# Two attention stages of a hybrid block, run one after the other or interleaved in one pipeline of 20 steps

## What is computed

```python
x = L0_attn_a_x                                    # (16, 512, 128)
x = x + attn_a(layernorm(x), w_qkv, w_out, b_out)  # 16 heads of 64
x = x + ffn(layernorm(x), W_r, W_k, W_v, mu_r, mu_k)
x = x + attn_b(layernorm(x), W_Q, W_K, W_V, W_O)   # 16 heads of 8, rotary
x = x + ffn(layernorm(x), W_r, W_k, W_v, mu_r, mu_k)

# attn_a, linear: q = softmax(q * 64**-0.5, over d), k = softmax(k, over tokens)
context = einsum('bnd,bne->bde', q, k); out = einsum('bde,bnd->bne', context, v)
return out @ w_out + b_out
# attn_b, full: q, k rotated
attn = softmax(einsum('bhqd,bhkd->bhqk', q, k) / sqrt(8)); ctx = einsum('bhqk,bhkd->bhqd', attn, v)
# ffn: x_prev is x shifted by one token
xr = mu_r * x + (1 - mu_r) * x_prev; xk = mu_k * x + (1 - mu_k) * x_prev
r = sigmoid(xr @ W_r); out = r * (square(relu(xk @ W_k)) @ W_v)
```

## Time and profile before

| | us |
|---|---|
| median of 3 runs (1165.8 to 1167.78) | 1166.34 |
| the profiled execution, its own time | 1165.81 |
| its span in the trace, first to last instruction | 1164.0 |
| busy: PE, ACT, DVE, POOL | 1019.4, 740.4, 676.2, 427.1 |

### The profile page before, as it was taken

The page is one execution under the profiler, slowest core; times in us unless marked ns, Lnnn a source line. Parts: engine busy times, 40 slices in busy tenths (PEclk is TensorE's granted clock), DMA queues, the critical chain, the costliest instruction groups (busy, mean ns, idle before and its releaser), DMA issues.

```text
span 1164.0 us, 23222 instructions
## 1 busy us (share of the span) xinstructions
PE 1019.4 (88%) x8311; PEld 582.1 (50%) x8311; DVE 676.2 (58%) x1620; ACT 740.4 (64%) x857; POOL 427.1 (37%) x338
## 2 busy tenths in 40 slices
PE   4999999999999999649998989998989999999993
PEld 3777777777777777532333333333333333333332
DVE  5788888888888888651334443444344434443334
ACT  3454444444444445318888888887888788878881
POOL 4555555555555555552302231223112311230000
PEclk9999999999999999969999999999999999999997
DMA  5011111111111111222332333233323332232211
GB/s 151 11 56 48 52 42 51 54 54 54 54 54 54 54 54 46 100 93 83 99 101 63 93 100 100 65 88 99 99 65 88 99 99 69 85 101 73 73 37 29
DMA packets 64184, 84.04 MB, mean 72 GB/s; under 512 B 12545, under 2 KB 39042, under 8 KB 64130
## 3 DMA queue, kind: packets, MB, share of 16 engines
q1 hardware_dynamic: 64130, 83.34, 23.8%
HBM read 28.77 MB, written 20.97 MB: 43 GB/s over the span
## 4 chain that ended last, share of the span: by engine, by line
PE 44%; DVE 20%; issue 17%; ACT 11%; POOL 3%; SPq 2%; DMA 2%; DVEq 0%; ACTq 0%; POOLq 0%
PE PS L1227 11%; ACT work L576 9%; PE PS L1208 9%; PE PS L945 5%; DVE work L609 4%; PE PS L950 3%; DVE q_sum L648 3%; PE PS L1056 3%; PE PS L952 3%; PE PS L951 3%; DVE st L591 2%; PE PS L1017 2%; DVE qk_norm L722 2%; PE PS L1065 1%; DMA qkv_back<-qkv_scratch 1%
## 5 line engine op out<-in xcount | busy, mean ns | idle before, releaser
L576 ACT ACTIVATE work<-PS 128x1024 f32<-128x1024 f32 x512 | 489.2, 1026 | 103.7 <-PE PS L1208 102.2
L1227 PE MATMUL PS<-work,v 128*32 128x512 f32 x2048 | 273.6, 606 | 1.1 <-ACT work L576 1.1
L1208 PE MATMUL PS<-q_st,k_st 32*128 32x512 f32 x1024 | 203.3, 498 | 40.6 <-ACT work L576 32.8
L1208 PEld LDWEIGHTS PS<-q_st,k_st 32*128 32x128 f32 x1024 | 80.1, 182 | 207.7 <-ACT work L576 167.9
L342 POOL TENSOR_TENSOR work<-work,q_rcp 128x1024 f32<-128x1024 f32 x64 | 122.3, 1912 | 89.8 <-DVE q_rcp L652 89.8
L331 POOL TENSOR_TENSOR rs<-ve,half_neg 128x4 f32<-128x4 f32 x64 | 66.1, 1033 | 240.2 <-DVE ve L602 240.2
L466 ACT ACTIVATE work<-PS 128x1024 f32<-128x1024 f32 x64 | 65.6, 1026 | 137.5 <-PE PS L952 137.5
L404 POOL TENSOR_TENSOR v<-qkv_back,one 128x512 f32<-128x512 f32 x16 | 16.6, 1040 | 265.7 <-PE PS L1227 265.7
L950 PE MATMUL PS<-work_r,h1h 128*128 128x512 f32 x256 | 109.1, 426 | 5.2 <-POOL h1l L337 3.4
L952 PE MATMUL PS<-work_r,h1l 128*128 128x512 f32 x256 | 102.0, 399 | 0.0
L951 PE MATMUL PS<-work_r,h1h 128*128 128x512 f32 x256 | 101.7, 397 | 0.0
(11 more groups left out here) (145 smaller groups left out, 1557.8 us busy)
## 6 DMA issues: line engine op xcount, KB each, us to landing
qkv_scratch<-qkv_sb SPq DMA_DIRECT2D x16, 768.0 KB, 3.2
qkv_back<-qkv_scratch SPq DMA_DIRECT2D x16, 768.0 KB, 4.6
work<-in_attn_a_x SPq DMA_DIRECT2D x32, 256.0 KB, 3.1
x_scratch<-x SPq DMA_DIRECT2D x16, 256.0 KB, 2.1
k_st<-k_hi SPq DMA_DIRECT2D x64, 64.0 KB, 2.1
k_st<-k_lo SPq DMA_DIRECT2D x64, 64.0 KB, 2.1
q_st<-q_hi SPq DMA_DIRECT2D x64, 64.0 KB, 2.1
q_st<-q_lo SPq DMA_DIRECT2D x64, 64.0 KB, 2.1
```

The costliest lines, as they stand in the source:

```text
L576: act.activation(probs[s % NC][:, 2 * t:2 * t + 2, :], PS[:, 2 * t:2 * t + 2, :], ACT.Exp).then_inc(s_exp.sem, 1)
L1208: mm = pe.matmul(PS[:, h, :], k_st[g % 2][rows, kc * P:(kc + 1) * P], q_st[g % 2][rows, :], start=True, stop=not guarded, tile_position=(3 ...
L1227: mm = pe.matmul(PS[32 * h:32 * h + 32, 4 + u, :], v_flat[p][:, kc, at:at + 32], probs[kc][:, h, :], start=(n % 8 == 0), stop=(n % 8 == 7) ...
```

## The change

Both halves become one loop (`fused`, 20 steps). Step i works on batch a = i (projections of attention A), s = i-1 (end of attention A, first feed-forward layer), l = i-2 (q, k, v of attention B, rotation, split), b = i-3 (scores and weighted values of attention B) and e = i-4 (its output, second feed-forward layer). Steps 3 to 15 have both a and b. Every step has 16 units. Unit n on PE is: one half of a projection (three products into the one bank 4), all four score tiles (banks 0 to 3) behind one wait, the weighing of the values of unit n-1 (bank 6), and then "the other product" of that unit, from a list written out by hand, in banks 4, 5 or 7. ACT does one exp of 128x512 and one of 128x2048 in a unit. Steps without b use four banks for the projections in turn; steps without a (16 to 18) make the scores in pairs, as before.

Because only eight banks exist, bank 4 serves the projections and six other products in a step; each is followed by a wait, ahead of the next projection, for the DVE instruction that empties it. q, k, v of attention B stay in SBUF (the copy back from DRAM goes; the store stays, for the branch of large norms). The mixtures of the feed-forward layers are now made from SBUF: ACT copies (`h_copy`), POOL subtracts (`difference`), DVE combines (`mix`). POOL squares k (was DVE), DVE takes relu (was ACT), DVE copies h1 and adds the rotation's parts (were ACT and POOL). The norms of q and k are judged in step 18; their branch now repeats attention B after the loop in the case of large norms only. E tiles of attention A have two buffers instead of four, and the exp results of attention B two instead of four.

```diff
-def over_batches(eng, step, n, tail, last=1):
...
+        def iterations(eng, step):
+            for i in range(5):
+                step(i, i % 2)
+            with eng.Fori(5, 13, 2) as i:
+                step(i, 1)
+                step(i + 1, 0)
+            for i in range(13, FUSED):
+                step(i, i % 2)
...
+            def exp_half(a, n, alone):
+                c, r = n // 4, n % 4
+                if r == 0:
...
+                    hold(act, c_mm, a, c - 1)
+                hold(act, ph_mm, a, n + 1)
+                bank = n % 4 if alone else 4
+                act.activation((EQ, EK)[r // 2][c % 2][:, (r % 2) * 512:(r % 2) * 512 + 512], PS[:, bank, :], ACT.Exp)\
+                   .then_inc(ph_exp.sem, 1)
+
+            def exp_scores(z, b, n):
+                hold(act, z["pv"], b, n - 1)
+                hold(act, z["s_mm"], b, n + 1)
+                act.activation(probs[n % 2], PS[:, 0:4, :], ACT.Exp).then_inc(z["s_exp"].sem, 1)
...
+            def proj_half(a, p, n, alone):
...
+                hold(pe, ph_exp, a, n - 3 if alone else n)
+                bank = n % 4 if alone else 4
...
+                halves(PS[:, bank, :], (h1h[p][:, tok], h1l[p][:, tok]), (wqk_hi[:, cols], wqk_lo[:, cols]))\
+                    .then_inc(ph_mm.sem, 1)
...
+            def scores(z, b, n):
+                g, kc = n // NC, n % NC
+                if kc == 0:
+                    stacks_there(z, b, g)
+                hold(pe, z["s_exp"], b, n)
+                for h in range(4):
+                    rows = slice(32 * h, 32 * h + 32)
+                    mm = pe.matmul(PS[:, h, :], k_st[g % 2][rows, kc * P:(kc + 1) * P], q_st[g % 2][rows, :],
+                                   start=True, stop=True, tile_position=(32 * h, 0))
+                mm.then_inc(z["s_mm"].sem, 1)
...
+                for n in range(16):
+                    if A:
+
+                        if B and n == 0:
+                            hold(pe, f1["relu"], l)
+                        if E and n == 3:
+                            hold(pe, z["ct_sb"], e)
+                        if B and n == 9 and there(a + 1):
+                            hold(pe, h1_sb, a + 1)
+                        if E and n == 11:
+                            hold(pe, f2["relu"], e)
+                        if B and n == 12:
+                            hold(pe, z["u_norm"], b, 2)
+                        if E and n == 13:
+                            hold(pe, f2["x"], e, 1)
+                        if B and n == 14:
+                            hold(pe, f1["relu"], s)
+                        proj_half(a, p, n, not B)
+                    if B and A:
+                        scores(z, b, n)
+                    if B and not A:
+                        scores_split(z, b, n)
+
+                    if B and n >= 1:
+                        weigh_values(z, b, n - 1, 1 - p)
+                    if E and n == 0:
+                        weigh_values(z, e, 15, p)
...
```

More of the change, by code:

```diff
@@ L78, in sig @@
             return Signal(ctx, nc, name, per)
[L82 to L96, removed]
@@ L230, in hybrid_block, with batches @@
+        def batches(eng, step):
+            step(0)
+            with eng.Fori(1, NB, 1) as j:
+                step(j)
         block = ctx.enter_context(nc.Block())
@@ new lines, in _ @@
+            pool.wait_ge(a_known.sem, a_known.at(0))
+            with pool.If(pool.value_load(bounded_a[0:1, 0:1], min_val=0, max_val=1) == 1):
+                iterations(pool, fused)
+            with pool.Else():
+                for j in range(NB):
+                    guarded_a(j)
+                    if there(j + 1):
+                        guarded_head(j + 1, (j + 1) % 2)
+            pool.wait_ge(b_known.sem, b_known.at(0))
+            with pool.If(pool.value_load(bounded_b[0:1, 0:1], min_val=0, max_val=1) == 0):
+                batches(pool, guarded_b)
@@ new lines, in guarded_a, with guarded_b @@
+            def guarded_a(j):
+                for c in range(NC):
+                    exp_q(j, c)
+                    exp_k(j, c)
+                t_copy(j)
+                m_copy(j)
+                h_copy(ffn[0], j)
+                gates(ffn[0], j)
+                hold(act, qkv_st, j - 1)
+                for c in range(NC):
+                    p_copy(j, c)
+            def guarded_b(i):
+                for n in range(16):
+                    exp_scores(att[1], i, n)
+                h_copy(ffn[2], i)
+                gates(ffn[2], i)
@@ new lines, in guarded_a @@
+            def guarded_a(j, p):
+                k_maxima(j)
+                k_shift(j)
+                for c in range(NC):
+                    q_shift(j, c)
+                    hold(dve, q_exp, j, c + 1)
+                    q_sums(j, c)
+                c_norm(j)
+                add_x1(j)
+                ln_norm(1, j, x1, hn)
+                mix(ffn[0], j)
+                relu(ffn[0], j, 4)
+                end_ffn1(j)
+                ln_norm(2, j, x2, h3)
+                split_h3(j)
@@ new lines, in guarded_b @@
+            def guarded_b(i):
+                z, f = att[1], ffn[2]
+                rope_sum(z, i)
+                split_kq(z, i, 0)
+                split_kq(z, i, 1)
+                for u in range(2):
+                    maxima(i, 2 * u)
+                    maxima(i, 2 * u + 1)
+                    pv_copy(z, i, u)
+                    normalise(z, i, u, 7)
+                cT_copy(z, i)
+                add_x3(z, 4, i)
+                ln_norm(4, i, x3, hn)
+                mix(f, i)
+                relu(f, i, 4)
+                gate_v(f, i, 4)
+                hold(dve, z["out_st"], i - 1)
+                add_gated(f, i, x3, out_sb)
```

1577 lines of the change are left out of this document (834 added, 743 removed).

## The result

The changed kernel takes **1181.28 us** (median of 4 runs, 1180.99 to 1182.74) against 1167.06 for the kernel before on the same chip: a ratio of 1.0125, 95% interval 1.0107 to 1.0142. It is 1.25% slower; 1128 us had been forecast, 3.3% faster. The profiled execution spans 1179.4 us, 52.9 more than the forecast sum of 1126.5.

The account below looks back on a forecast made before the run. PE taken as bound in the first half (27.2 of 29.6 us), neither PE nor ACT cleanly in the second. 22 + 76 + 871 + 127.5 + 30 = 1126.5, with 1.8 around it 1128 us; range 1095 to 1160.

Parts of the forecast that it names:

- Part 1: Between the two halves: the 45 us hole, chain of the last batch alone, all to go in one loop.
- Part 2: PE's products in a full step (3 to 15): first half 27.2, second 30.6, switches 2.5; sum 60.3 us.
- the 7.8 us of turn taking: Second half's step today: 38.4 less 30.6 us of products; PE and ACT alternate, four tiles together end it.
- Part 3: What PE waits for in a full step: six bank 4 waits 6.0 us, late DVE 0.7; full step 67.0.
- Half a us of air: DVE's slack from the end of `ffn_v` in unit 15 to unit 2's transposes: through at 9.3, PE at 9.8.
- Part 4: Whole kernel: set-up 22, steps 0-2 76, 13 full steps 871, steps 16-18 127.5, step 19 30; 1128 us.
- sign of being right: Steps 62 to 69 us apart, six PE waits totalling 6 us, no clock under 0.9 between 93 and 1100.
- Rival 2: DVE late beside POOL in full steps: 5 us more a step, 72 us; 1193 us in all; chance 0.20.
- Rival 1: Cheaper loop body: full step 63.0 us by less work, free switches, smaller waits; 1076 us; chance 0.20.
- Rival 3: Second split slips over 2 us, first scores wait for q stack: 2 us a step, 69.0, 1154; chance 0.06.
- Rival 4: The change doesn't do what it says: the branch for large weights would be taken; chance 0.01.
- rule of the lock: Against the change: each of ten exposed DVE groups could wait out a POOL instruction; the sum would be Rival 2's.

Follow-up runs that it names:

- e11: Kernel of e9 with two DVE swaps: relu of e ahead of `rope_sum`, first split of k ahead of `gate_v`; 1056.88 us (0.9054).
- e4: Changed kernel with all score tiles in pairs, an exp for each pair, in the full steps too; 1183.11 us (1.0126).
- e1: Changed kernel with all 20 steps written out, no hardware loop; 1161.8 us (0.9947).
- e12: Kernel of e11 with POOL's `difference` ahead of the split of h1 in steps 0 to 2; 1051.53 us (0.9005).
- e8: Kernel of e7 with POOL's square last in the step, DVE taking the norms' maximum a step later; 1103.21 us (0.9446).
- e9: Kernel of e8 with the mixture of e reading one input from PSUM bank 7 in place of SBUF; 1086.33 us (0.9301).
- e3: Changed kernel with POOL's square cut to 4 elements and the judging of the norms left out; 1155.12 us (0.9894).
- e6: Changed kernel with `gate_v` of e ahead of the mixture of s in DVE's order; 1157.62 us (0.9911).
- e7: Changed kernel with steps written out, weighing behind the other product in the six bank 4 units, and `gate_v` ahead of the mixture; 1134.06 us (0.9704).

## Why the prediction was wrong, by its own steps

**Part 1, the hole: right.** The 45 us of the earlier trace rows are gone; in the window of steps 4 to 15 PE is busy 89%, and no stretch between steps 3 and 16 is the chain of one batch alone.

**Part 2, PE's own work of 60.3: right.** e11, where hardly anything holds PE up, measures 59.6. But "all sixteen units at 0.44 is what four at once buys" names the wrong part: e4 makes the scores in pairs and loses nothing that can be measured. By e4 and steps 16 to 18 the 7.8 us of turn taking were bought by the projections between the units. And the 251 waits and 159 us read from the earlier trace rows are those of the weight loads, which run beside the products; PE's own waits for the exp are 97 and 32.8 us, shown above. The 7.8 stands on the sum of the products, not on that row.

**Part 3, waits of 6.7 and a full step of 67.0: the sum right, its makeup wrong.** Bank 4 costs 6.45 us a step (6.0 forecast), and the nine undisturbed steps average 67.0. But 1.85 of the 6.45 (22.2 in 12) are the one wait for `gated`, behind a mixture that the lock makes three times as long, and the clock's fall behind that wait costs another 1.3 (0.87 on the weighing; 0.42 on the transposes, 0.91 from start to start against 0.49 at 580.01) which I hadn't counted. PE's 59.6, the waits' 6.45 and this 1.3 make 67.3. "Half a us of air" I had looked for at the step's start; the tight place was ahead of unit 13, where the two instructions of the late mixture stand before the one that empties bank 4.

**Part 4, where it failed.** The forecast gained 38 us; four terms of the sum were 64 us too small, and step 3, 11 us shorter than forecast, gave some of it back.
- *The hardware loop at nothing, 19.5 us (e1).* The prediction has no term for it. A row to ask about was there: a body of two full steps is some 1000 products (6210 in 12 steps) with as many weight loads, twice the bodies of before, and the loop of the first half brought in nearly no instructions.
- *Steps 0 to 2 at 76 (71 to 86); they take 103.5.* This is the largest error. I wrote that the order is that of the full step and gave 5 us for it, without following DVE and POOL through it. In the full steps that order lies beside 60 us of PE's work; here there are no scores to lie beside. PE is idle 24.7 us where it was idle 3.2 in the 71 us of before, and busy 10.9 us more for about as many products (692 and 713), at a mean clock of 0.84 against 0.98. So of the 32.5 us more 21.6 are waits, and the rest goes with the slower clock. PE's waits in the changed kernel, 22 to 181 us:

```profile
PE PS L1050 <- DVE k_lo L790: 8.0, 1, 8.0
PE PS L1148 <- DVE mixed_k L748: 4.2, 1, 4.2
```

  Behind the first, in step 2, stands POOL: DVE waits 6.1 us for its difference, and then the mixture meets the square (2.36 us). The edits up to e12 got back 9.5 of the 27.5, 7.9 of it those of e11 and e12, which only change orders; for the rest it isn't shown which wait or order sets it.
- *Step 3 at 67; it takes 56.* It has scores but no batch e yet, and I priced it as a full step. This error went the other way, by luck.
- *Steps 16 to 18 at 127.5 (120 to 140); they take 142.3.* Step 16 takes 56.4 and step 17 46.0, for 48 and 41 forecast. With the orders of DVE and POOL changed and one mixture read from PSUM, e12 needs 131.3, step 16 of it 47.6. So most of what was missing was lateness, and 4 us are still open.
- *Step 19 at 30; it takes 32.1,* and 33.3 in e12, so nothing that I tried touches it. Its waits are for hn (5.05), mixed_r (3.38) and k_act (2.04), on the chain of one batch. The tail of before, 28 us, waited 4.96 for hn and 2.94 for its mixture, and not for the square. Not tried further.

The prediction's own sign of being wrong asked for a full step outside 62 to 72 or more than 150 us in steps 16 to 18. Neither came, since the error lay in steps 0 to 2 and in the jumps. Its sign of being right failed: the clock was under 0.9 behind each jump and behind the wait for `gated`.

**The rivals.** Rival 2 ended on the right side (slower) for a reason that was mostly another. Its mechanism is real and larger than I held it: getting the long instructions out of each other's way gave 31 us (e8) and 17 us (e9), and undoing the worst meeting gave 26 (e3). Its signs came too, a mixture of 2.05 us in the mean and waits of 2 us. But a full step took 67.0 and not 72; the lock was paid inside what I had called the price of bank 4. Rival 1 was wrong: no full step was under 65.6. Rival 3 was wrong in the full steps; one wait of 2.47 us for a q stack stands at the start of step 18. Rival 4 was wrong.

**The rule of the lock held.** The mixture of s takes 2.37 us beside POOL's square (1.89) and 0.75 without it, and ends 0.56 us after POOL's instruction. That agrees with what the Trainium skill says on its page SBUF — State Buffer, section Who interferes with whom: an exclusive lock for the whole instruction. But my count of ten groups with POOL at work 45% of the time was the wrong model. The order of both engines is fixed, and so the same pairs meet in nearly every step: both mixtures, the norm of a+1 (2.70 us for 1.11) and the norms' maximum (0.93 for 0.29). The adds, the rotation's sum and the other norms hardly do.

## What to carry to other kernels

When stages are merged into one pipeline, price its ends by following the slower engines through them with the new order, since an order made for the full step has no cover there. When a bank is awaited, put work that doesn't need it (here the weighing) between the product that fills it and the wait, but first see that the emptying instruction isn't itself late: the same move gave 6 us with DVE late and 40 with DVE on time. Write a long body out: the jump cost 6.5 us each time. Whether a shorter body would do as well wasn't run. And when one instruction is moved out of another's way, see what it meets next (e9).

## What the runs showed of the hardware

- A jump back over a body of two steps leaves PE idle 4.2 us at a time while the instruction queues move 5 or 6 packets in 10 us, against 0 to 2 elsewhere; written out, nearly as many packets in all (75 for 88) came without such a wait. With the slow clock behind it (0.65 in the mean of 8 us), 6.5 us.
- DVE's instruction of 128x512 with two inputs in SBUF takes 0.75 us; 2.37 when POOL's instruction of 1.89 us started 0.08 us before it, and 2.00 when one of 1.52 us did. Both end 0.56 us after POOL's. With one of the inputs in PSUM it is 0.75 us every time (x16, 746 to 749 ns), beside the same instruction of POOL.
- Behind PE's wait of 1.95 us the products ran at half the clock, and behind 0.86 us at the same place at the full one (e6). At another place it was half behind 2.34 us (e7) and full behind 1.19 us (e8). So the price of such a wait is more than its length: 1.3 us more at either place.
- Four score tiles behind one wait, or two and two, made no difference once the exp was done in time: 1181.28 and 1183.11 us, ratios 1.0125 and 1.0126.
